# Row maxima of attention scores taken from the transposed scores by 32x32 block transposes

## The chip, the cores and the metric

The kernel runs on one core of a Trainium2 chip. The metric is the device time of one execution in microseconds (us). The core has five engines that work side by side, each through its own queue in order, and that wait for one another through semaphores: TensorE (PE, matmuls into the accumulation memory PSUM), VectorE (DVE), ScalarE (ACT), GpSimd (POOL), and SyncE (SP), which here issues the transfers. PEld is TensorE's load of the stationary operand, which overlaps its matmuls.

## The reference

Two attention layers, one after the other, on 256 positions (16 x 16) of 192 channels. Each layer normalises its input in groups of six channels, computes attention with 12 heads of 16 channels and adds the result to its input. The second layer adds a low-rank term (`A`, `B`) to the weights of q and v. Cut to what matters here:

```python
q, k, v = heads(xn @ W + b)                       # 12 heads, 256 positions, 16 channels
attn = (q * scale) @ k.T                          # 256 x 256 for each head
attn = attn + rel_h[..., :, None] + rel_w[..., None, :]   # from q and the row/column of the key
attn = softmax(attn, axis=-1)
x = x + (attn @ v) @ Wo + bo
```

The softmax subtracts the maximum over the keys from each query's row before the exponential.

## The kernel before

`LAYERS` = 2, `NH` = 12 heads, handled in `PAIRS` = 6 pairs; `NG` = 3 groups of 4 heads for the product with v; `TT` = 2 tiles of 128 positions. PSUM has 8 banks of 512 columns. For every head the operands `qs` and `ks` have 128 rows, which hold q and k in high and low parts and the relative positions, so that one matmul of 128 rows gives the finished scores.

The order of all work is written out by hand: each engine has one list of instructions, and the semaphores are named after what they announce. In the attention part of a layer:

- PE, `scores(l, p)`: scores of pair p with queries as rows (lines 579 on), two heads, two tiles each, into banks 0 and 1 (`S_BANK`). They serve for the maxima alone.
- DVE, `maxima(l, p)`: for each head a reduction of 512 columns to the two tiles' row maxima, negated, into `nm` (line 395).
- POOL, `split_maxima(l, p)`: splits `nm` into a high and a low part in `nmhl` (lines 254 and 256), so that a rounded 32-bit format (fp32r) carries it exactly.
- PE, `turn_max(l, p)`: two matmuls with the identity turn them into rows, in bank 7 (`NM_BANK`, line 605). Bank 7 holds "r" rows of group 2 before (`R_BANK`), so the first waits for the last "r" move.
- ACT, `max_rows(l, p)`: copies these 4 rows into `nmt`.
- PE, `scores_t(l, p)`: the scores again, with keys as rows (line 593), into two pairs of banks in turn (`ST_BANK` = [3, 5]). From the third pair on it waits for the exponentials that empty the banks (`p_sb`).
- PE, `add_max(l, p)`: two matmuls of 512 columns with `ones4` add the negated maxima to the transposed scores (line 615).
- ACT, `probabilities(l, p)`: the exponential of 1024 columns into `pt` (line 316).
- PE, `probs_v(l, g)`: product with v for a group (line 633), then DVE or ACT copies it (`out_columns`, `ot`), `turn_out` turns it back (line 643), and DVE's `normalise` divides by the row sums.

Ahead of this part stand the group norm (DVE's statistics L425, POOL's power L208, DVE's L446 into `xn`), the q, k products (L716), copies into `zq` and `zk` in high parts by ACT and low parts by DVE (L471), the relative positions (L736), and the moves of "k", "q" and "r" rows from PSUM into `ks` and `qs` (ACT's in the order of `ACT_MOVES`, line 268; DVE's, line 380). `keep_busy(n)` issues n small matmuls that have no use but to occupy TensorE. At the start, POOL and DVE fill constants (`ident`, `gavg`, `onehot`, `ones4`, `nmt` and others).

The functions and their callers:

Of the kernel before, what the change touches and what calls it, by code (L numbers as in the profile page):

```python
# [33 lines left out]
def attention_layers(nc, x, w_in0, w_out0, w_in1, w_out1, lora, rel, out):  # L34
# [4 lines left out]
    with ctx:  # L39
# [3 lines left out]
        def sem(name):  # L43
# [17 lines left out]
        ones4_raw = sb("ones4_raw", [P, 2, P])  # L61
        ones4 = sb("ones4", [P, 2, P], F32R)
# [26 lines left out]
        nm = sb("nm", [P, PAIRS, 2, TT])  # L89
        nmhl = sb("nmhl", [P, PAIRS, TT, 2, 2], F32R)  # L90
        nmt = sb("nmt", [P, PAIRS, T], F32R)
# [14 lines left out]
        zeroed, made_ident, made_gavg, made_ones4, made_ones, made_va = (sem(n) for n in (  # L106
            "zeroed", "made_ident", "made_gavg", "made_ones4", "made_ones", "made_va"))
# [4 lines left out]
        (gn_ps, qk_ps, v_ps, rel_ps, k_ps, q_ps, r_ps, s_ps, st_ps, nmt_ps, o_ps, oq_ps, ont_ps,  # L112
         y_ps, lora_ps) = (sem(n) for n in (
            "gn_ps", "qk_ps", "v_ps", "rel_ps", "k_ps", "q_ps", "r_ps", "s_ps", "st_ps", "nmt_ps",
            "o_ps", "oq_ps", "ont_ps", "y_ps", "lora_ps"))

        (warmed, xt_sb, relhi_sb, z_hi, rr_hi_sb, moved_act, nmt_sb, p_sb, ont_sb,
         ot_act, res_act) = (sem(n) for n in (
            "warmed", "xt_sb", "relhi_sb", "z_hi", "rr_hi_sb", "moved_act", "nmt_sb", "p_sb",
# [18 lines left out]
        S_BANK = [0, 1]  # L138
        ST_BANK = [3, 5]
        O_BANK, NM_BANK = [2, 2, 1], 7  # L140
# [10 lines left out]
        BUSY_WITH_MAXIMA = [8, 5]  # L151
# [52 lines left out]
        def _(pool):  # L204
# [25 lines left out]
            for n, steps in enumerate(([-1, 0], [0, -1], [-1, 0], [0, -1])):  # L230
# [5 lines left out]

            pool.memset(va[:, :, :, D:VW], 0.0).then_inc(zeroed, 1)
            pool.memset(ones4_raw[:, :, :], 1.0).then_inc(zeroed, 1)
            pool.wait_ge(zeroed, 11)
            pool.memset(va[:, :, :, D:D + 1], 1.0).then_inc(made_va, 1)  # L240

            pool.affine_select(out=ones4_raw[:, :, :], in_=ones4_raw[:, :, :],
                               compare_op=ALU.is_ge, fill=0.0, base=0, pattern=[[-2, 2], [0, P]],
                               channel_multiplier=1).then_inc(zeroed, 1)
            pool.wait_ge(zeroed, 12)
# [20 lines left out]
        def _(act):  # L266
# [40 lines left out]
            def max_rows(l, p):  # L307

                if l == 0 and p == 0:
                    act.wait_ge(nmt_zero, 1)  # L310
# [521 lines left out]
```

## Time and profile before

| | |
|---|---|
| median of 3 runs | 81.52 us (81.52 to 81.66) |
| profiled execution | 81.54 us |
| its span | 79.5 us |
| PE busy | 69.9 us (88%) |
| PEld busy | 56.0 us (70%) |
| ACT busy | 51.9 us (65%) |
| DVE busy | 45.7 us (58%) |
| POOL busy | 11.8 us (15%) |
| granted TensorE clock, mean | 0.998 of full speed |

The span runs from the first to the last instruction of the profile; the execution's own time has 2.0 us around it. A group row reads: line, engine, operation, result and operands, shapes, number | busy us, mean ns of one | idle time of that engine just before them and what ended it. Matmuls are pipelined: one lasts longer than the distance to the next.

### The profile page before, as it was taken

The numbers are of one execution on the slowest core, as the hardware profiler recorded it, in microseconds if no ns is written. First come the engines' busy times: TensorE is split into PE (matmuls) and PEld (weight loads), VectorE is DVE, ScalarE is ACT, GpSimd is POOL, SyncE is SP. The second block draws the span as 40 slices with busy tenths as digits, with TensorE's granted clock in tenths as the row PEclk, the third lists the DMA queues.
The fourth block names the chain that finished last, engine by engine and source line by source line (L and its number), as shares of the span: only waits on it lengthen the run. The fifth ranks groups of instructions, "written<-read, shape, count | busy, mean of one in ns | idle before, by whom it ended". The sixth has DMA issues, their size and how long they took to land.

```text
span 79.5 us, 1633 instructions
## 1 busy us (share of the span) xinstructions
PE 69.9 (88%) x632; PEld 56.0 (70%) x632; DVE 45.7 (58%) x107; ACT 51.9 (65%) x98; POOL 11.8 (15%) x46
## 2 busy tenths in 40 slices
PE   4976989999978999979999999999878999988750
PEld 4955869998656975824768889999656994834630
DVE  4863999767846685422254649759576666323210
ACT  5429797999979787561330067799979787581420
POOL 5876400000121111000001100000031122000000
PEclk9999999999999999999999999999999999999999
DMA  0968000000000000000000000000000000000003
GB/s 13 278 167 264 12 0 8 0 0 0 0 4 0 8 4 0 0 0 0 0 8 0 0 0 0 0 0 0 8 0 0 0 0 0 0 8 0 0 0 99
DMA packets 1543, 1.75 MB, mean 22 GB/s; under 512 B 312, under 2 KB 1146, under 8 KB 1536
## 3 DMA queue, kind: packets, MB, share of 16 engines
q1 hardware_dynamic: 1536, 1.66, 7.2%
q8 instruction: 5, 0.08, 0.4%
q14 instruction: 2, 0.02, 0.1%
HBM read 1.46 MB, written 0.20 MB: 21 GB/s over the span
## 4 chain that ended last, share of the span: by engine, by line
PE 74%; DVE 10%; ACT 6%; issue 5%; POOL 1%; DVEq 0%; ACTq 0%
PE ps L736 10%; PE ps L633 8%; PE ps L579 7%; PE ps L593 7%; PE ps L615 6%; PE ps L716 6%; PE ps L503 5%; PE ps L564 4%; ACT qs L268 3%; PE ps L643 3%; PE ps L605 2%; PE ps L692 2%; PE ps L536 2%; PE ps L671 2%; PE ps L681 2%
## 5 line engine op out<-in xcount | busy, mean ns | idle before, releaser
L395 DVE TENSOR_REDUCE nm<-ps 128x2 f32<-128x512 f32 x24 | 15.5, 686 | 7.3 <-PE ps L579 7.1
L316 ACT ACTIVATE pt<-ps 128x1024 f32<-128x1024 f32 x12 | 12.3, 1024 | 1.4
L268 ACT ACTIVATE qs<-ps 64x512 fp32r<-64x512 f32 x20 | 11.8, 589 | 0.4
L503 PE MATMUL ps<-busy 128*128 128x128 bf16 x112 | 9.4, 243 | 1.5 <-DVE busy L365 1.1
L503 PEld LDWEIGHTS ps<-busy 128*128 128x128 bf16 x112 | 7.9, 112 | 2.5 <-DVE busy L365 1.0
L579 PE MATMUL ps<-ks,qs 128*128 128x256 f32 x48 | 8.9, 300 | 0.7 <-DVE nm L395 0.3
L736 PEld LDWEIGHTS ps<-zq,table 128*64 128x64 f32 x128 | 7.9, 138 | 0.7 <-issue 0.5
L736 PE MATMUL ps<-zq,table 128*64 128x48 f32 x128 | 8.0, 216 | 0.2 <-DVE zq L471 0.2
L254 POOL CAST nmhl<-nm 128x4 fp32r<-128x4 f32 x12 | 2.2, 187 | 40.1 <-DVE nm L395 40.1
L615 PE MATMUL ps<-nmt,ones 128*128 128x512 f32 x24 | 8.1, 418 | 0.1
L593 PE MATMUL ps<-qs,ks 128*128 128x256 f32 x48 | 8.1, 291 | 0.0
L579 PEld LDWEIGHTS ps<-ks,qs 128*128 128x128 f32 x48 | 6.7, 189 | 1.8 <-issue 0.9
L593 PEld LDWEIGHTS ps<-qs,ks 128*128 128x128 f32 x48 | 6.7, 189 | 1.3 <-issue 0.8
L268 ACT ACTIVATE nmt<-ps 4x256 fp32r<-4x256 f32 x12 | 4.4, 370 | 4.1 <-PE ps L605 3.9
L716 PE MATMUL ps<-xn,win 97*128 97x256 f32 (+1 forms) x24 | 5.7, 387 | 0.8 <-DVE xn L446 0.8
L633 PE MATMUL ps<-pt,va 128*32 128x256 f32 x96 | 6.4, 385 | 0.0
L268 ACT ACTIVATE ks<-ps 64x512 fp32r<-64x512 f32 x10 | 5.7, 589 | 0.1
L478 DVE TENSOR_TENSOR rr_lo<-ps,rr_hi 64x384 fp32r<-64x384 f32 x8 | 4.2, 548 | 2.4 <-ACT rr_hi L268 2.4
L268 ACT ACTIVATE zq<-ps 64x256 fp32r<-64x256 f32 x6 | 2.3, 378 | 5.1 <-PE ps L716 5.0
L716 PEld LDWEIGHTS ps<-xn,win 97*128 97x128 f32 (+1 forms) x24 | 4.4, 189 | 1.5 <-DVE xn L446 1.0
L386 DVE RECIPROCAL rinv<-ps 128x8 f32<-128x8 f32 x6 | 1.2, 208 | 6.0 <-PE ps L643 6.0
L268 ACT ACTIVATE rr_hi<-ps 64x384 fp32r<-64x384 f32 x8 | 3.6, 480 | 1.5 <-PE ps L736 1.4
(94 smaller groups left out, 104.5 us busy)
## 6 DMA issues: line engine op xcount, KB each, us to landing
win<-in_w_in_dram SPq DMA_DIRECT2D x4, 216.0 KB
xt<-in_x_dram SPq DMA_DIRECT2D x1, 192.0 KB, 2.7
wout<-in_w_out_dram SPq DMA_DIRECT2D x2, 96.0 KB
out_dram<-res SPq DMA_DIRECT2D x1, 192.0 KB, 2.0
wout<-in_w_out_dram SPq DMA_DIRECT2D x2, 48.0 KB
rel_raw<-in_rel_dram SPq DMA_DIRECT2D x1, 62.0 KB, 2.9
win<-in_w_in_dram SPq DMA_DIRECT2D x2, 2.2 KB
wout<-in_w_out_dram SPq DMA_DIRECT2D x2, 0.8 KB
```

The source lines that it names most:

```text
L268: return act.activation(dst, src, ACT.Copy, scale=scale)
L316: act.activation(pt[:, p, :, :, :].rearrange("p a k t -> p a (k t)"), ps[:, ST_BANK[p % 2]:ST_BANK[p % 2] + 2, :], ACT.Exp, scale=SCALE[l] ...
L395: dve.tensor_reduce(nm[:, p, a, :], ps[:, S_BANK[a], :].rearrange("p (t k) -> p t k", k=T), AX.X, ALU.max, negate=True).then_inc(max_sb, 1)
L478: dve.tensor_tensor(rel_dst(rr_lo, which, half), rel_src(which, half), rel_dst(rr_hi, which, half).bitcast(F32), ALU.subtract).then_inc(rr ...
L503: mm(ps[:, bank, 0:P], busy[:, :], busy[:, :], start=True, stop=True)
L564: last = mm(ps[:, R_BANK[g], u * T:(u + 1) * T], pick[:, 2 * u:2 * u + 2, :].rearrange("p j n -> p (j n)"), rr[:, g, :], start=(part == 0 ...
L579: last = mm(ps[:, S_BANK[a], t * T:(t + 1) * T], qs[:, 2 * p + a, t * P:(t + 1) * P], ks[:, 2 * p + a, :], start=True, stop=True)
L593: mm(ps[:, ST_BANK[p % 2] + a, t * T:(t + 1) * T], ks[:, 2 * p + a, t * P:(t + 1) * P], qs[:, 2 * p + a, :], start=(t == 0), stop=False, s ...
L615: last = mm(ps[:, ST_BANK[p % 2] + a, :].rearrange("k (t q) -> k t q", q=T), ones4[:, a, :], nmt[:, p, :].unsqueeze(1).to_broadcast([P, TT ...
L633: last = mm(ps[32 * j:32 * j + 32, O_BANK[g], 0:T], va[:, t, G4 * g + j, :], pt[:, 2 * g + j // 2, j % 2, t, :], start=(t == 0), stop=(t = ...
L716: last = mm(ps[:, m, 0:T], win[l][0:rows, ic, m * P:(m + 1) * P], xn[0:rows, ic, :], start=(ic == 0), stop=(ic == 1))
L736: last = mm(ps[0:64, b, c:c + NG * HW], table[l][:, part, which, HW - 1 - i:2 * HW - 1 - i, :].rearrange("p r j -> p (r j)"), moving, star ...
```

## The change

The maxima are taken from the transposed scores. The scores with queries as rows (`scores` before), their banks, and `nmt` with its ACT copies are gone. The new `scores(l, p)` computes what `scores_t` did, into three pairs of banks in turn. `block_tops(l, p, a)` lets VectorE transpose each 32x32 block of one head's scores and reduce it, so that `top` holds for every query the maximum over 32 keys. `turn_tops` turns 16 columns of `top` on PE into bank 7; `maxima` takes the maximum over the 8 blocks of keys, negated, into `nm` (16 rows: head and block of 32 queries; 32 columns). POOL splits `nm` into `nm_hl`, and a new third POOL operation multiplies it with the 0/1 table `place` into `shift`, 256 columns, with every value in its query's column and zeros elsewhere. `subtract_max` adds it to the scores with `ones_rows`. `O_BANK` becomes [2, 0, 1], and the product of group 1 no longer waits for `on` of group 0. `BUSY_WITH_MAXIMA` goes from [8, 5] to 8. At the start DVE computes `place` and `head_rows` and does not clear `nmt`; POOL waits for the normalised input of layer 0 before it clears `va`, `nm_hl` and `shift`, and copies `ones_rows`; the selects of `ones4` go.

```diff
-        S_BANK = [0, 1]
-        ST_BANK = [3, 5]
-        O_BANK, NM_BANK = [2, 2, 1], 7
+        ST_BANK = [0, 3, 5]
+        O_BANK, NM_BANK = [2, 0, 1], 7
-        BUSY_WITH_MAXIMA = [8, 5]
+        BUSY_WITH_MAXIMA = 8
 # POOL
+            pool.wait_ge(xn_sb, NC)
             pool.memset(va[:, :, :, D:VW], 0.0).then_inc(zeroed, 1)
+            pool.memset(nm_hl[:, :, :].bitcast(F32), 0.0).then_inc(shift_zero, 1)
+            pool.memset(shift[:, :, :, :].bitcast(F32), 0.0).then_inc(shift_zero, 1)
+            pool.wait_ge(made_place, 2)
+            pool.tensor_copy(ones_rows[:, :, :], head_rows[:, :].unsqueeze(2).to_broadcast([P, 2, P])
+                             ).then_inc(ones_sb, 1)
             def split_maxima(l, p):
+                n = PAIRS * l + p + 1
+                pool.wait_ge(nm_sb, n)
+                pool.tensor_copy(nm_hl[0:16, p, :], nm[:, p, :]).then_inc(nm_hi, 1)
+                pool.wait_ge(nm_hi, n)
+                pool.tensor_tensor(nm_hl[32:48, p, :], nm[:, p, :], nm_hl[0:16, p, :].bitcast(F32),
                                    ALU.subtract).then_inc(nm_lo, 1)
+                pool.wait_ge(nm_lo, n)
+                if l == 1:
+                    pool.wait_ge(st_ps, p + 1)
+                pool.tensor_tensor(shift[0:48, p, :, :],
+                                   nm_hl[:, p, :].bitcast(F32).unsqueeze(1).to_broadcast([48, 8, 32]),
+                                   place[0:48, :].unsqueeze(2).to_broadcast([48, 8, 32]),
+                                   ALU.mult).then_inc(shift_sb, 1)
 # ACT
-                for n in range(3, 13):
-                    move(l, n)
-                max_rows(l, 0)
-                for n in range(13, 15):
+                for n in range(3, 15):
                     move(l, n)
                 for p in range(PAIRS):
                     probabilities(l, p)
-                    if p == 0:
-                        max_rows(l, 1)
-                    if p + 2 < PAIRS:
-                        max_rows(l, p + 2)
 # DVE
-            dve.memset(nmt[:, :, :].bitcast(F32), 0.0).then_inc(nmt_zero, 1)
+            dve.tensor_reduce(place[:, :], ident[:, :].rearrange("p (x b) -> p b x", b=8),
+                              AX.X, ALU.add).then_inc(made_place, 1)
+            dve.tensor_reduce(head_rows[:, :],
+                              ident[:, 0:64].rearrange("p (s x) -> p s x", s=2)[:, :, 0:16].rearrange(
+                                  "p s (a b) -> p a s b", a=2), AX.XY, ALU.add).then_inc(made_place, 1)
+            def block_tops(l, p, a):
+                dve.wait_ge(s_ps, NH * l + 2 * p + a + 1)
+                if l == 1:
+                    dve.wait_ge(top_ps, p + 1)
+                dve.tensor_reduce(top[:, p, :, a, :],
+                                  ps[:, ST_BANK[p % 3] + a, :].rearrange("p (t b q) -> p t b q", t=TT, q=32),
+                                  AX.X, ALU.max, apply_transpose=True).then_inc(top_sb, 1)
             def maxima(l, p):
+                dve.wait_ge(top_ps, PAIRS * l + p + 1)
+                if l == 1:
+                    dve.wait_ge(nm_lo, p + 1)
+                dve.tensor_reduce(nm[:, p, :],
+                                  ps[0:16, NM_BANK, 0:T].rearrange("p (t b q) -> p q t b", t=TT, q=32),
+                                  AX.XY, ALU.max, negate=True).then_inc(nm_sb, 1)
-                for p in range(PAIRS):
-                    maxima(l, p)
+                block_tops(l, 0, 0)
+                block_tops(l, 0, 1)
+                for p in range(1, PAIRS):
+                    block_tops(l, p, 0)
+                    if p != 3:
+                        maxima(l, p - 1)
+                    block_tops(l, p, 1)
+                    if p == 2:
+                        maxima(l, 2)
                 out_columns(l, 0)
+                maxima(l, 5)
                 normalise(l, 0)
 # PE
+            def scores(l, p):
+                if p == 0:
                     pe.wait_ge(made_keys, 4)
                     moved(l, *(m for g in range(NG) for m in both("k", g)))
                     pe.wait_ge(v_sb, TT * l + 2)
+                elif p >= 3:
+                    pe.wait_ge(p_sb, PAIRS * l + p - 2)
                 moved(l, *both("q", p // 2), *both("r", p // 2))
                 for a in range(2):
                     for t in range(TT):
+                        last = mm(ps[:, ST_BANK[p % 3] + a, t * T:(t + 1) * T],
+                                  ks[:, 2 * p + a, t * P:(t + 1) * P], qs[:, 2 * p + a, :],
+                                  start=(t == 0), stop=(t == 1), skip_group_check=True)
+                    last.then_inc(s_ps, 1)
+            def turn_tops(l, p):
                 if p == 0:
                     moved(l, *both("r", 2))
                 else:
+                    pe.wait_ge(nm_sb, PAIRS * l + p)
+                pe.wait_ge(top_sb, NH * l + 2 * p + 2)
                 for t in range(TT):
+                    last = pe.transpose(ps[0:16, NM_BANK, t * P:(t + 1) * P],
+                                        top[:, p, t, :, :].rearrange("p a b -> p (a b)"), ident[:, :])
+                last.then_inc(top_ps, 1)
+            def subtract_max(l, p):
+                pe.wait_ge(ones_sb, 1)
+                pe.wait_ge(shift_sb, PAIRS * l + p + 1)
                 for a in range(2):
+                    last = mm(ps[:, ST_BANK[p % 3] + a, :].rearrange("k (t q) -> k t q", q=T), ones_rows[:, a, :],
+                              shift[:, p, :, :].rearrange("p b q -> p (b q)").unsqueeze(1).to_broadcast([P, TT, T]),
                               start=False, stop=True, skip_group_check=True)
                 last.then_inc(st_ps, 1)
 # PE, order of a layer's attention part
+                for p in range(3):
+                    scores(l, p)
+                turn_tops(l, 0)
+                turn_tops(l, 1)
+                subtract_max(l, 0)
+                turn_tops(l, 2)
                 moved(l, *both("q", 2))
+                keep_busy(BUSY_WITH_MAXIMA, bank=O_BANK[0])
+                subtract_max(l, 1)
+                scores(l, 3)
+                subtract_max(l, 2)
+                scores(l, 4)
+                turn_tops(l, 3)
+                scores(l, 5)
+                turn_tops(l, 4)
+                subtract_max(l, 3)
+                probs_v(l, 0)
+                turn_tops(l, 5)
+                subtract_max(l, 4)
+                turn_out(l, 0)
+                probs_v(l, 1)
+                subtract_max(l, 5)
+                turn_out(l, 1)
                 probs_v(l, 2)
```

## Rows read from the trace of the kernel before

**Rows 1.** The page: busy time by engine, TensorE's granted clock in 40 slices.

```profile
PE 69.9 (88%) x632; PEld 56.0 (70%) x632; DVE 45.7 (58%) x107; ACT 51.9 (65%) x98; POOL 11.8 (15%) x46
...
PEclk9999999999999999999999999999999999999999
```

**Rows 2.** Timeline, layer 0, attention: start us, us, engine, line, operation.

```profile
18.77 4.28 ACT L268 ACTIVATE qs<-ps 64x512 fp32r<-64x512 f32 x7
...
23.16 0.28 PE L605 MATMUL ps<-ident_r,nmhl 128*4 128x128 f32 x2 [0.54 <-issue]
...
25.03 1.02 ACT L316 ACTIVATE pt<-ps 128x1024 f32<-128x1024 f32 x1
...
33.02 2.18 ACT L316 ACTIVATE pt<-ps 128x1024 f32<-128x1024 f32 x2
...
36.06 1.07 PE L633 MATMUL ps<-pt,va 128*32 128x256 f32 x16
```

**Rows 3.** The chain that ended last, layer 1: start us, us, what.

```profile
72.28 1.04 PE ps L633 x16
```

**Rows 4.** Groups by line with shapes apart.

```profile
L395 DVE TENSOR_REDUCE nm<-ps 128x2 f32<-128x512 f32 x24 | 15.5, 686 | 7.3 <-PE ps L579 7.1
...
L579 PE MATMUL ps<-ks,qs 128*128 128x256 f32 x48 | 8.9, 300 | 0.7 <-DVE nm L395 0.3 <-issue 0.2
...
L615 PE MATMUL ps<-nmt,ones 128*128 128x512 f32 x24 | 8.1, 418 | 0.1
...
L268 ACT ACTIVATE nmt<-ps 4x256 fp32r<-4x256 f32 x12 | 4.4, 370 | 4.1 <-PE ps L605 3.9
...
L605 PE MATMUL ps<-ident_r,nmhl 128*4 128x128 f32 x24 | 3.4, 222 | 1.3 <-issue 1.1
...
L400 DVE COPY ot<-ps 128x256 f32<-128x256 f32 x4 | 1.7, 425 | 4.7 <-PE ps L633 4.7
...
L256 POOL TENSOR_TENSOR nmhl<-nm,nmhl 128x4 fp32r<-128x4 f32 x12 | 2.4, 200 | 1.0
...
L254 POOL CAST nmhl<-nm 128x4 fp32r<-128x4 f32 x12 | 2.2, 187 | 40.1 <-DVE nm L395 40.1
...
L232 POOL TENSOR_SCALAR_AFFINE_SELECT onehot<-onehot 128x256 f32<-128x256 f32 x4 | 2.1, 534 | 0.6
...
L650 PE MATMUL ps<-ident,on 128*64 128x128 f32 x4 | 0.8, 285 | 0.2 <-DVE on L388 0.2
...
L214 POOL TENSOR_SCALAR_AFFINE_SELECT ident<-ident 128x128 f32<-128x128 f32 x1 | 0.3, 289 | 0.2 <-POOL ident L212 0.2
```

**Rows 5.** The chain that ended last: behind a reduction (L395); one pair's scores.

```profile
20.83 0.14 issue
...
27.63 0.48 PE ps L579 x4
```

**Rows 6.** Timeline, start of layer 0.

```profile
0.80 0.38 SPq L162 DMA_DIRECT2D xt<-in_x_dram  x1
...
2.42 1.34 DVE L370 MEMSET nmt<- 128x1536 f32 x1 [0.27 <-issue]
...
3.98 0.74 DVE L425 BATCH_NORM_STATS2 stats<-xt 96x6 f32<-96x256 f32 x2
...
6.99 2.30 ACT L268 ACTIVATE ks<-onehot 64x768 fp32r<-64x768 f32 x3
...
7.43 1.19 DVE L446 TENSOR_SCALAR xn<-xt,gmean,rstd 96x256 f32<-96x256 f32 x2 [0.89 <-POOL rstd L208]
...
10.43 1.32 DVE L471 TENSOR_TENSOR zq<-ps,zq 64x256 fp32r<-64x256 f32 x3
...
11.90 2.02 PE L736 MATMUL ps<-zq,table 128*64 128x48 f32 x32 [0.25 <-DVE zq L471]
```

**Rows 7.** Timeline, start of layer 1, the same L446.

```profile
44.25 0.73 DVE L446 TENSOR_SCALAR xn<-xt,gmean,rstd 96x256 f32<-96x256 f32 x2 [0.37 <-POOL rstd L208]
```

**Rows 8.** DMA issues: KB each, median us from issue to landing.

```profile
xt<-in_x_dram SPq DMA_DIRECT2D x1, 192.0 KB, 2.7
```

More of the change, by code:

```diff
@@ L60, in attention_layers @@
         pick_rl = sb("pick_rl", [P, G4, 64], F32R)
-        ones4_raw = sb("ones4_raw", [P, 2, P])
-        ones4 = sb("ones4", [P, 2, P], F32R)
+        place = sb("place", [P, 8])
+        head_rows = sb("head_rows", [P, 2])
+        ones_rows = sb("ones_rows", [P, 2, P], F32R)
         win = [sb(f"win{l}", [CH + 1, NC, 3 * C]) for l in range(LAYERS)]
@@ L88, in attention_layers @@
         ks = sb("ks", [P, NH, T], F32R)
-        nm = sb("nm", [P, PAIRS, 2, TT])
-        nmhl = sb("nmhl", [P, PAIRS, TT, 2, 2], F32R)
-        nmt = sb("nmt", [P, PAIRS, T], F32R)
+        top = sb("top", [P, PAIRS, TT, 2, 8])
+        nm = sb("nm", [16, PAIRS, 32])
+        nm_hl = sb("nm_hl", [48, PAIRS, 32], F32R)
+        shift = sb("shift", [P, PAIRS, 8, 32], F32R)
         pt = sb("pt", [P, PAIRS, 2, TT, T])
@@ L235, in _ @@
             inverse_deviation(0)
+            pool.wait_ge(xn_sb, NC)
             pool.memset(va[:, :, :, D:VW], 0.0).then_inc(zeroed, 1)
[L238 to L239 removed]
+            pool.wait_ge(zeroed, 10)
             pool.memset(va[:, :, :, D:D + 1], 1.0).then_inc(made_va, 1)
[L242 to L244 removed]
@@ L305, in move @@
                 copy(dst, src).then_inc(moved_act, 1)
-            def max_rows(l, p):
-                if l == 0 and p == 0:
-                    act.wait_ge(nmt_zero, 1)
-                act.wait_ge(nmt_ps, PAIRS * l + p + 1)
-                copy(nmt[0:4, p, :], ps[0:4, NM_BANK, 0:T]).then_inc(nmt_sb, 1)
             def probabilities(l, p):
@@ L316, in probabilities @@
                 act.activation(pt[:, p, :, :, :].rearrange("p a k t -> p a (k t)"),
-                               ps[:, ST_BANK[p % 2]:ST_BANK[p % 2] + 2, :], ACT.Exp,
+                               ps[:, ST_BANK[p % 3]:ST_BANK[p % 3] + 2, :], ACT.Exp,
                                scale=SCALE[l]).then_inc(p_sb, 1)
@@ L567, in relative_rows @@
                 last.then_inc(r_ps, 1)
-            def scores(l, p, heads=(0, 1)):
-                if p == 0 and 0 in heads:
+            def scores(l, p):
+                if p == 0:
                     pe.wait_ge(made_keys, 4)
@@ L573, in scores @@
                     pe.wait_ge(v_sb, TT * l + 2)
+                elif p >= 3:
+                    pe.wait_ge(p_sb, PAIRS * l + p - 2)
                 moved(l, *both("q", p // 2), *both("r", p // 2))
-                for a in heads:
-                    if p >= 1:
-                        pe.wait_ge(max_sb, NH * l + 2 * p + a - 1)
-                    for t in range(TT):
-                        last = mm(ps[:, S_BANK[a], t * T:(t + 1) * T],
-                                  qs[:, 2 * p + a, t * P:(t + 1) * P], ks[:, 2 * p + a, :],
-                                  start=True, stop=True)
-                    last.then_inc(s_ps, 1)
@@ L604, in turn_max @@
                 for t in range(TT):
-                    last = mm(ps[0:4, NM_BANK, t * P:(t + 1) * P],
-                              nmhl[:, p, t, :, :].rearrange("p a s -> p (a s)"), ident_r[:, :],
-                              start=True, stop=True)
-                last.then_inc(nmt_ps, 1)
-            def add_max(l, p):
-                if l == 0 and p == 0:
-                    pe.wait_ge(made_ones4, 1)
-                pe.wait_ge(nmt_sb, PAIRS * l + p + 1)
+                    last = pe.transpose(ps[0:16, NM_BANK, t * P:(t + 1) * P],
+                                        top[:, p, t, :, :].rearrange("p a b -> p (a b)"), ident[:, :])
```

76 lines of the change are left out of this document (10 added, 66 removed).

## The prediction

> **What bounds the kernel now.** I read the page first: TensorE (PE) is busy 88% of the span, VectorE (DVE) 58%, ScalarE (ACT) 65%, GpSimd (POOL) 15%, and the granted clock of TensorE is at full speed, its level of 2.4 GHz, in every slice [rows 1]. That suggests that PE work taken away is time won. The timeline of the attention loop is the test of it. In layer 0 the loop begins with the scores at about 19.6 us. The first turned maxima (L605) come only at 23.16, right after ACT's seventh copy of the stretch that began at 18.77 has ended at 23.05: bank 7, which they write, holds the last "r" rows until then. The first exponentials start at 25.03, the last two end at 35.20 (33.02 + 2.18), and the last `probs_v` starts at 36.06 [rows 2]. In layer 1 the same `probs_v` starts at 72.28 [rows 3], 36.2 us later. So the loop is 16.5 us long per layer, and I judge the change by one mark: when the last `probs_v` starts. What comes after it (copy, turns, projection) is not changed.
>
> **What is removed.** Per pair of heads, PE loses the four matmuls of `scores` (L579; 0.48 us per pair in the chain, 0.12 each, 2.9 us per layer [rows 5]), VectorE loses two reductions to 2 columns of 0.69 us each, ACT loses one 0.37 us copy of `nmt` (2.2 us per layer), and the filler loses 5 of 13 small matmuls (0.3 us) [rows 4]. ACT's copies of the last two "q" rows no longer stand behind the first `nmt` copy.
>
> **What is added, per pair.** (1) Two reductions with 32x32 transposes, 128x512 in each. The reduction of the same input takes 0.69 us [rows 4]; no row shows a transposing one. It reads the same 512 columns, so it cannot be cheaper than 0.69 unless columns stop counting; if a block has to fill before it drains and nothing overlaps, it is about twice the 0.53 us of streaming, 1.2 us. I take 0.72 (one block of 32 columns extra) because the row is the same operation on the same tile; ends 0.69 and 1.2. (2) Two PE transposes of `top`: the nearest form is the turn of `on` with few output columns (L650, 0.285 us each, a pair 0.41), against 0.28 for today's L605 pair. (3) A reduction of 256 columns on 16 partitions: as the 256-column copy from PSUM, 0.42 us; 0.30 at the least. (4) On POOL a copy and a subtraction of 32 columns where there were 4: 0.19 and 0.20 us today [rows 4], which I take as 0.22 and 0.25. (5) A new POOL multiplication into `shift`, 256 columns from two inputs. Selects of 256 columns take up to 0.53 us and one of 128 takes 0.29, which is 1.9 ns a column; 0.20 + 256 x 1.9 ns = 0.69 us. Bounds: 0.41 (a one-input pass of that width, from below) and 1.0 (two such passes). I take 0.69, since the second input has to be read as well. (6) `subtract_max` costs what `add_max` did, 0.68 us for its pair from the first start to the last end.
>
> The Trainium skill's page "GPSIMD Engine Reference", section 3.1, speaks against putting this step on GpSimd: it counts about 2.6 cycles per element for a two-input elementwise operation and 4,497 ns for 2,048 columns, about twice VectorE. [...] No row of this case shows the operation.
>
> **The new chain.** In place of maxima, split (0.47 us on POOL), turn, ACT copy, there is now: block maxima of two heads (1.4 us), +0.11, turn 0.41, maxima 0.42, POOL 0.22 + 0.08 + 0.25 + 0.08 + 0.69 = 1.32, +0.11, subtract 0.68, exponentials 1.02 [rows 4]. For the steps to PE I add 0.11 us, a little under the 0.14 us between the end of a reduction and the next matmul [rows 5], and 0.03 to the others. With the scores (0.5) a pair of banks is held for 6.1 us, and there are three pairs of banks, so a pair of heads comes every 2.0 us at best, as today (the six end 10.2 us after the first starts, so a step is 1.8). The change widens the ring from two to three pairs of banks, and the turn of one grows from 3.6 (two steps of 1.8) to 6.1 us.
>
> Walking layer 0 on the clock of the trace before (order of each engine as in the diff):
> - Scores 0 and 1 at 19.6 and 20.1, block maxima from 20.1. VectorE's queue then holds `maxima(0)`, and `turn_tops(0)` still waits for bank 7 until 23.05, so it starts at 23.16 as L605 does now. VectorE stands still from 22.1 to 23.6 with the rest of pairs 1 and 2 behind it.
> - `maxima(0)` ends at 24.05, POOL at 25.4, subtract 25.5 to 26.2, exponentials 0 from 26.2 to 27.3: 1.2 us later than now.
> - On PE `scores(3)` stands behind `subtract_max(1)`, which gets its shift at 27.2; scores 3 at 27.8, their block maxima end at 29.6, but `maxima(3)` stands behind the first block maxima of pair 4 (29.9 to 30.6). It ends at 31.0, POOL at 32.3, exponentials 3 run from 33.1.
> - Block maxima of pair 5 end at 33.4; `turn_tops(5)` stands behind `probs_v(0)` (32.9 to 33.9). `maxima(5)` ends at 34.85, POOL at 36.2, subtract at 37.0, exponentials 5 at 38.05, `probs_v(2)` starts at 38.2.
>
> So the mark moves from 36.06 to 38.2: 2.1 us per layer, 4.2 us for two. The PE work that went lay beside these waits and buys nothing; ACT's 2.2 us per layer as well.
>
> **The start of layer 0.** VectorE no longer clears `nmt` (1.34 us at 2.42), and does two reductions of about 0.15 instead. It would be ready for the statistics at about 3.1; their input was issued at 0.80 and landed 2.7 later, at 3.5 [rows 8], so they start at 3.57, not 3.98: 0.41 earlier. POOL now clears its tiles only after the normalised input is done. In layer 0, with POOL's memsets beside them, the two L446 take 1.19 us, in layer 1, with POOL still, 0.73 [rows 7]: the first is 0.25 shorter. ACT's first `zq` copy then comes at once after its one-hot copies end at 9.29 (6.99 + 2.30); three of them, 0.4 each, end at 10.5, and the third `zq` subtraction, which today ends at 11.75 (10.43 + 1.32) because VectorE came late to the row, ends at 10.95. PE's L736 starts at 11.1 in place of 11.90: 0.8 us gained [rows 6]. POOL's own new work there (a 1536-column clear, a copy) ends by 11 and nothing waits for it before 20.
>
> **Sum.** The profiled execution: 81.54 us, of which 79.5 are the span. 81.54 + 4.2 - 0.8 = 84.9. The median of the runs is 81.52, the same within 0.02.
>
> **Rivals.**
> - *PE bounds the loop, so its removed work counts* (faster). For: 88% busy, as the page has it. Per layer 2.9 + 0.3 of matmuls go and 6 x 0.13 of longer turns come: 2.4 us, twice, and 0.8: 75.9 at best, and anything up to 81.3 if part of it shows. It decides if the three links maxima, POOL and subtract together are some 0.8 us a pair shorter than the 2.4 above, so that the last exponentials end before 36.3. Against: even with POOL's multiplication at 0.20, as its 4-column row, my walk gives 82.7. Chance 0.09.
> - *The transposing reduction is about half speed* (1.0 to 1.2 us). VectorE then bounds: twelve of them a layer add 0.3 to 0.5 each, and the walk gives 88.4 at 1.0 and 92.0 at 1.2. Nothing in the rows speaks for or against it. Chance 0.12. The Trainium skill's "Vector Engine (DVE) Microarchitecture Reference", section 3.8, has the transposing front end sustain one element per cycle and lane; by that the reduction stays at 0.69 and the sum is 84.7. No row here shows it.
> - *POOL's links are cheap* (multiplication 0.41 to 0.45, maxima 0.30): 82.0 to 83.2, still slower. Chance 0.16.
> - *TensorE's clock falls to 1.2 GHz in the loop*: with fewer matmuls and fewer fillers PE stands idle up to 1.2 us at a time (23.6 to 24.9), and in the profile before the clock never left 2.4 GHz [rows 1], so no row prices it. With matmuls 0.12 us apart becoming 0.24 and all of PE's links doubling, the walk gives 94; a part of it 87 to 90. Chance 0.05. The Trainium skill's "TensorE: Matmul & The Clock Gate" (HAM oscillation) has long idle gaps lower the clock; the trace of before agrees only in that busy stretches keep it.
> - The forecast: chance 0.54, own range 83.2 to 86.6 (multiplication up to 0.9, reduction up to 0.85). No measurable change, within 0.2% (about what a measurement of this kernel can tell from nothing): 0.04, where several links are short at once.
>
> Faster 0.10 (the first rival and a little of the cheap links), same 0.04, slower 0.86. The range for 8 in 10 runs from 81.9 to 88.4: below it lies the first rival, above it the half-speed reduction.
>
> **What would show it.** The transposing reduction at 0.69 to 0.76; POOL's multiplication at 0.6 to 0.8 and POOL as a link of the chain that ended last; VectorE waiting for the first `turn_tops` from about 21.3 to 22.8 (0.8 earlier than on this clock); first exponentials at about 25.4 and last `probs_v` of layer 0 at 37.4; L736 first at 11.1; clock at full. I am wrong if the exponentials keep a step under 1.8 us, or if a step of POOL or of VectorE's new forms lies outside its bounds.

## The result and the profile after

The changed kernel takes 86.55 us (median of 4 runs, 86.27 to 89.18) against 81.52 before: 1.060 times as long, with a 95% interval of 1.056 to 1.064. The profiled execution took 86.37 us, 84.6 of them the span. Executions of one kernel do not all keep TensorE's clock here. So below I read stage lengths from profiled executions and name the granted clock beside the times.

The page after: span, busy time by engine, granted clock in 40 slices.

```profile
span 84.6 us, 1557 instructions
...
PE 68.7 (81%) x574; PEld 51.6 (61%) x574; DVE 48.6 (57%) x120; ACT 47.8 (57%) x86; POOL 20.3 (24%) x58
...
PEclk9999999999975999999999999999955579999999
```

[Rows 1] had 69.9 us of PE. 58 fewer matmuls on TensorE have made it busy for only 1.2 us less, because part of them ran at half speed: the digits of the clock fall to 5 twice, once in each layer's attention loop; before they were 9 throughout. In the chain that ended last (by engine, share of the span) TensorE has 44% where it had 74% before, and ScalarE 29% where it had 6%:

```profile
PE 44%; ACT 29%; DVE 8%; issue 5%; POOL 4%; DMA 4%; SPq 2%; POOLq 1%; DVEq 0%
```

Groups with shapes apart, the counterparts of [rows 4]:

```profile
L392 DVE TRANSPOSE_TENSOR_REDUCE top<-ps 128x16 f32<-128x512 f32 x24 | 15.8, 689 | 4.8 <-PE ps L593 4.6
L315 ACT ACTIVATE pt<-ps 128x1024 f32<-128x1024 f32 x12 | 12.3, 1024 | 16.5 <-PE ps L613 16.3
...
L613 PE MATMUL ps<-shift,ones_rows 128*128 128x512 f32 x24 | 10.3, 518 | 1.3 <-POOL shift L260 1.1
...
L593 PE MATMUL ps<-qs,ks 128*128 128x256 f32 x48 | 8.4, 306 | 3.0 <-ACT qs L274 2.1 <-ACT pt L315 0.6 <-issue 0.2
...
L260 POOL TENSOR_TENSOR shift<-nm_hl,place 48x256 fp32r<-48x256 f32 x12 | 7.3, 608 | 1.0 <-POOL nm_hl L255 0.2
...
L605 PE MATMUL ps<-ident,top 128*16 128x128 f32 x24 | 5.4, 313 | 4.0 <-DVE top L392 3.1 <-ACT qs L274 1.0
L400 DVE TENSOR_REDUCE nm<-ps 16x32 f32<-16x256 f32 x12 | 4.8, 404 | 4.8 <-PE ps L605 4.8
...
L255 POOL TENSOR_TENSOR nm_hl<-nm,nm_hl 16x32 fp32r<-16x32 f32 x12 | 2.9, 243 | 1.0
...
L253 POOL CAST nm_hl<-nm 16x32 fp32r<-16x32 f32 x12 | 2.4, 199 | 40.2 <-DVE nm L400 40.2
```

The transposing reduction takes 0.689 us, as the plain one did (0.686). POOL's multiplication takes 0.608, the maxima 0.404, the widened copy and subtraction 0.199 and 0.243. The means of L613 (0.518) and L605 (0.313) hide two speeds: a part of them ran at the low clock.

The timeline of layer 0's loop (start us, us, engine, line, operation), the counterpart of [rows 2]:

```profile
22.84 0.39 PE L605 MATMUL ps<-ident,top 128*16 128x128 f32 x2 [0.49 <-ACT qs L274]
...
25.17 1.19 PE L613 MATMUL ps<-shift,ones_rows 128*128 128x512 f32 x2
...
26.40 1.02 ACT L315 ACTIVATE pt<-ps 128x1024 f32<-128x1024 f32 x1 [2.38 <-PE ps L613]
...
27.45 0.81 PE L613 MATMUL ps<-shift,ones_rows 128*128 128x512 f32 x2
28.10 0.63 PE L593 MATMUL ps<-qs,ks 128*128 128x256 f32 x4
...
32.98 1.07 PE L627 MATMUL ps<-pt,va 128*32 128x256 f32 x16
33.09 1.02 ACT L315 ACTIVATE pt<-ps 128x1024 f32<-128x1024 f32 x1 [2.61 <-PE ps L613]
...
33.98 0.39 PE L605 MATMUL ps<-ident,top 128*16 128x128 f32 x2
...
35.53 0.61 POOL L260 TENSOR_TENSOR shift<-nm_hl,place 48x256 fp32r<-48x256 f32 x1
...
36.28 0.70 PE L613 MATMUL ps<-shift,ones_rows 128*128 128x512 f32 x2 [0.23 <-POOL shift L260]
...
37.02 1.02 ACT L315 ACTIVATE pt<-ps 128x1024 f32<-128x1024 f32 x1 [1.12 <-PE ps L613]
...
38.10 1.07 PE L627 MATMUL ps<-pt,va 128*32 128x256 f32 x16 [0.90 <-ACT pt L315]
```

The first turn is at 22.84, the first exponentials at 26.40, the last `probs_v` at 38.10, where before they stood at 23.16, 25.03 and 36.06.

Busy time by stretch. A row gives the stretch and its length, then the busy time of PE, PEld, DVE, ACT and POOL, each with its number of instructions, then the granted clock (1.00 is full speed), the DMA share and GB/s. First after, then before for the stretch that leads up to the first exponentials:

```profile
20.60:22.80 2.20, 0.77 (x5) 0.53 (x4) 1.27 (x3) 2.12 (x4) 0.00 (x0) 1.00 0.01 4
22.80:28.00 5.20, 3.80 (x18) 2.31 (x19) 3.08 (x6) 2.21 (x3) 2.59 (x9) 0.67 0.00 0
28.00:38.00 10.00, 8.12 (x64) 4.42 (x62) 6.71 (x15) 5.08 (x5) 3.71 (x10) 1.00 0.01 2
...
61.40:69.00 7.60, 6.31 (x27) 4.42 (x28) 4.39 (x8) 3.32 (x5) 3.15 (x9) 0.55 0.01 2
```

```profile
20.80:25.00 4.20, 3.27 (x18) 2.25 (x18) 3.10 (x6) 3.62 (x7) 0.77 (x4) 1.00 0.01 2
```

Between 20.60 and 22.80 TensorE is busy for 0.77 of 2.20 us, where the kernel before had 3.27 of 4.20. After that the clock falls to its lower level, 1.2 GHz: the mean is 0.67 over 5.2 us in layer 0 and 0.55 over 7.6 us in layer 1. With 0.5 as the lower level these means give an estimate of 3.4 and 6.8 us spent there.

The start of layer 0, the counterpart of [rows 6]:

```profile
3.84 0.75 DVE L431 BATCH_NORM_STATS2 stats<-xt 96x6 f32<-96x256 f32 x2 [0.94 <-DMA xt<-in_x_dram]
...
5.96 0.40 ACT L274 ACTIVATE rel_hi<-rel_raw 128x62 fp32r<-128x62 f32 x2 [3.07 <-DMA rel_raw<-in_rel_dram]
...
7.30 0.73 DVE L452 TENSOR_SCALAR xn<-xt,gmean,rstd 96x256 f32<-96x256 f32 x2 [0.89 <-POOL rstd L209]
7.42 2.30 ACT L274 ACTIVATE ks<-onehot 64x768 fp32r<-64x768 f32 x3
7.77 2.86 PE L710 MATMUL ps<-xn,win 97*128 97x256 f32 x12 [0.58 <-DVE xn L452]
...
9.75 1.19 ACT L274 ACTIVATE zq<-ps 64x256 fp32r<-64x256 f32 x3
10.16 1.32 DVE L477 TENSOR_TENSOR zq<-ps,zq 64x256 fp32r<-64x256 f32 x3 [0.49 <-ACT zq L274]
...
11.63 0.56 PE L730 MATMUL ps<-zq,table 128*64 128x48 f32 x7 [0.35 <-DVE zq L477]
```

The input landed 3.0 us after its issue in this execution instead of 2.7, and the statistics start at 3.84. The two L452 take 0.73, as worked out. ScalarE's first `zq` copy is at 9.75: its row of nine operations begins when the relative positions' input has landed, at 5.96 (5.52 in the profile before). L730 starts at 11.63, 0.27 earlier than before, where 0.8 was forecast. In the profile before, the same copy waited for TensorE's products instead:

```profile
9.73 1.18 ACT L268 ACTIVATE zq<-ps 64x256 fp32r<-64x256 f32 x3 [0.44 <-PE ps L716]
```

To place the 5.1 us between the spans, I use four marks per layer from the timelines. "Loop" is from the first scores to the last `probs_v`.

| | before | after |
|---|---|---|
| first scores, layer 0 | 19.61 | 19.44 |
| loop, layer 0 | 16.45 | 18.66 |
| between the loops | 19.94 | 19.79 |
| loop, layer 1 | 16.21 | 19.47 |
| from the last `probs_v` to the end of the span | 7.29 | 7.24 |

The loops account for 2.21 + 3.26 us; the rest gives 0.4 back.

### The profile page after: what moved, and what is told of

The parts are those of the page before. It is cut to its first block, busy times and chain, and to the rows that moved or that the text cites. A ratio compares the mean times of both kernels' runs of the same rounds, so it can differ in the third digit from the quotient of the medians.

```text
span 84.6 us, 1557 instructions
## 1 busy us (share of the span) xinstructions
PE 68.7 (81%) x574; PEld 51.6 (61%) x574; DVE 48.6 (57%) x120; ACT 47.8 (57%) x86; POOL 20.3 (24%) x58
## 4 chain that ended last, share of the span: by engine, by line
PE 44%; ACT 29%; DVE 8%; issue 5%; POOL 4%; DMA 4%; SPq 2%; POOLq 1%; DVEq 0%
ACT qs L274 11%; PE ps L613 10%; ACT ks L274 9%; PE ps L627 5%; PE ps L730 5%; PE ps L517 4%; DMA rel_raw<-in_rel_dram 4%; PE ps L605 4%; PE ps L710 3%; ACT rr_hi L274 3%; PE ps L593 3%; ACT pt L315 2%; DVE top L392 2%; DVE nm L400 2%; POOL shift L260 2%
## 5 line engine op out<-in xcount | busy, mean ns | idle before, releaser
L315 ACT ACTIVATE pt<-ps 128x1024 f32<-128x1024 f32 x12 | 12.3, 1024 | 16.5 <-PE ps L613 16.3
L392 DVE TRANSPOSE_TENSOR_REDUCE top<-ps 128x16 f32<-128x512 f32 x24 | 15.8, 689 | 4.8 <-PE ps L593 4.6
L253 POOL CAST nm_hl<-nm 16x32 fp32r<-16x32 f32 x12 | 2.4, 199 | 40.2 <-DVE nm L400 40.2
L613 PE MATMUL ps<-shift,ones_rows 128*128 128x512 f32 x24 | 10.3, 518 | 1.3 <-POOL shift L260 1.1
L605 PE MATMUL ps<-ident,top 128*16 128x128 f32 x24 | 5.4, 313 | 4.0 <-DVE top L392 3.1
L730 PEld LDWEIGHTS ps<-zq,table 128*64 128x64 f32 x128 | 7.9, 138 | 0.8 <-issue 0.6
L730 PE MATMUL ps<-zq,table 128*64 128x48 f32 x128 | 8.0, 216 | 0.3 <-DVE zq L477 0.3
L400 DVE TENSOR_REDUCE nm<-ps 16x32 f32<-16x256 f32 x12 | 4.8, 404 | 4.8 <-PE ps L605 4.8
L260 POOL TENSOR_TENSOR shift<-nm_hl,place 48x256 fp32r<-48x256 f32 x12 | 7.3, 608 | 1.0 <-POOL nm_hl L255 0.2
L613 PEld LDWEIGHTS ps<-shift,ones_rows 128*128 128x128 f32 x24 | 4.6, 241 | 3.8 <-issue 3.8
L605 PEld LDWEIGHTS ps<-ident,top 128*16 128x16 f32 x24 | 1.4, 88 | 7.4 <-issue 3.0
L627 PEld LDWEIGHTS ps<-pt,va 128*32 128x32 f32 x96 | 2.5, 109 | 4.4 <-ACT pt L315 2.3
```

The lines of the kernel that those rows point to most:

```text
L260: pool.tensor_tensor(shift[0:48, p, :, :], nm_hl[:, p, :].bitcast(F32).unsqueeze(1).to_broadcast([48, 8, 32]), place[0:48, :].unsqueeze(2) ...
L315: act.activation(pt[:, p, :, :, :].rearrange("p a k t -> p a (k t)"), ps[:, ST_BANK[p % 3]:ST_BANK[p % 3] + 2, :], ACT.Exp, scale=SCALE[l] ...
L392: dve.tensor_reduce(top[:, p, :, a, :], ps[:, ST_BANK[p % 3] + a, :].rearrange("p (t b q) -> p t b q", t=TT, q=32), AX.X, ALU.max, apply_t ...
L400: dve.tensor_reduce(nm[:, p, :], ps[0:16, NM_BANK, 0:T].rearrange("p (t b q) -> p q t b", t=TT, q=32), AX.XY, ALU.max, negate=True).then_i ...
L605: last = pe.transpose(ps[0:16, NM_BANK, t * P:(t + 1) * P], top[:, p, t, :, :].rearrange("p a b -> p (a b)"), ident[:, :])
L613: last = mm(ps[:, ST_BANK[p % 3] + a, :].rearrange("k (t q) -> k t q", q=T), ones_rows[:, a, :], shift[:, p, :, :].rearrange("p b q -> p ( ...
```

## The experiments

**Fillers in the gaps** (`fill`). Small matmuls in unused columns of bank 7, partitions 64 on.

```diff
                 turn_tops(l, 0)
+                for _ in range(18): mm(ps[64:P, NM_BANK, T:T + P], busy[:, 0:64], busy[:, :], start=True, stop=True)
                 turn_tops(l, 1)
+                for _ in range(8): mm(ps[64:P, NM_BANK, T:T + P], busy[:, 0:64], busy[:, :], start=True, stop=True)
                 subtract_max(l, 0)
```

> The changed kernel with 26 filler matmuls per layer in the two gaps of TensorE behind the first and the second turn of the block maxima (64 columns of weights, 128 columns moved, into an unused part of bank 7). If the fall of TensorE's clock to 1.2 GHz in the loop costs the part that the walk of links does not explain (about 1.6 us), the clock stays at 1.00 and the time is 84.6 to 85.4 us. If the clock is a symptom only and the waits set the pace, 86.3 to 86.6. If TensorE's occupied time bounded the loop, it would be slower than the changed kernel, 87.5 or more.

The four executions: 84.24 and 84.14 at a clock of 1.00, 87.33 and 86.91 at 0.96. The windows of the profiled one (84.24), same stretches as above:

```profile
22.80:28.00 5.20, 4.80 (x48) 3.37 (x46) 3.56 (x7) 2.78 (x4) 3.15 (x9) 1.00 0.01 3
...
61.40:69.00 7.60, 6.49 (x54) 4.48 (x51) 5.96 (x11) 3.36 (x4) 3.90 (x12) 1.00 0.00 0
```

The loops are 18.10 and 18.18 us long. With the clock held, the changed kernel is thus 2.1 us faster in spite of 52 more matmuls, so the clock costs 0.56 + 1.29 us in the loops of the profile after, and TensorE's occupied time is not what bounds them. It is still 1.030 times as long as the kernel before (1.024 to 1.037). The other two executions show that fillers of this number do not hold the clock each time. The forecast of 84.6 to 85.4 was 0.4 too high. The second group of fillers stands in the way of the first `subtract_max`: it starts at 25.09, though its shift is ready at 24.80, so the fillers may cost up to 0.2 us of the loop (an estimate).

**Without the multiplication** (`no_mult`). This kernel leaves the maxima unsubtracted (`shift` stays zero) and takes a hundredth of the exponentials' scale.

```diff
-                pool.wait_ge(nm_lo, n)
-                ...
-                pool.tensor_tensor(shift[0:48, p, :, :], ..., ALU.mult).then_inc(shift_sb, 1)
-                pe.wait_ge(shift_sb, PAIRS * l + p + 1)
+                pe.wait_ge(nm_lo, PAIRS * l + p + 1)
```

> The changed kernel without GpSimd's multiplication into shift: the maxima are not subtracted (shift stays zero) and the exponentials take a hundredth of the scale. The chain of links has three multiplications in a row per layer (pairs 0, 3 and 5), each 0.61 us and 0.07 of handover: 6 x 0.68 = 4.1 us less, 82.4 us, and more if TensorE's gaps become short enough to keep the clock (81). If the loop were bound by TensorE's work or by ScalarE, less than 1.5 us would come back: 85 or more.

85.03 us (84.67 to 85.86), clock 0.93 to 0.96: a miss, against 82.4. The loop of layer 0 took 18.73 us, no less than with the multiplication; that of layer 1 took 18.25, 1.2 less. Windows of its layer 0:

```profile
24.00:26.00 2.00, 1.44 (x4) 0.67 (x4) 1.80 (x4) 0.21 (x1) 0.65 (x3) 0.50 0.00 0
26.00:28.00 2.00, 1.88 (x12) 1.68 (x13) 0.41 (x1) 0.81 (x1) 0.44 (x2) 0.50 0.00 0
28.00:30.00 2.00, 2.00 (x8) 1.70 (x7) 1.02 (x2) 1.02 (x1) 0.00 (x0) 0.50 0.00 0
```

The clock is at its lower level from 24 to 30 us. TensorE is busy there for 1.44, 1.88 and 2.00 of each 2.00 us, so from 26 on its own matmuls at half speed fill the time and shorter links can buy little. Clock and link are mixed in this run, and it does not give the price of the link.

**The kernel before without its fillers** (`before_nofill`).

```diff
-        BUSY_WITH_MAXIMA = [8, 5]
+        BUSY_WITH_MAXIMA = [0, 0]
```

> The kernel before without its 13 filler matmuls per layer in the attention loop. If fillers are what holds the clock there, the granted clock falls to about 0.95 and the time rises by 1 us or more, to 82.5 or above. If the loop's own matmuls suffice, the clock stays at 1.00 and the time is 81.0 to 81.6, as 0.6 us of filler per layer lies partly on the chain.

81.55 us, ratio 0.9995 (0.9957 to 1.0032). The page of this kernel:

```profile
span 79.5 us, 1581 instructions
...
PE 69.2 (87%) x606; PEld 54.9 (69%) x606; DVE 45.7 (57%) x107; ACT 51.9 (65%) x98; POOL 11.8 (15%) x46
...
PEclk9999999999999999999999999999999999999999
```

The clock stays up without the fillers, in all ten executions (0.999 or 1.000); the old loop's own matmuls keep it. The kernel before with its fillers, timed beside it, lost the clock in 4 of 13 executions (85.67 to 85.85 us at 0.95 and 0.96), so these fillers are no guarantee. And 0.7 us of TensorE work gone (69.9 to 69.2) change the span by nothing. In the profile before, the fillers stood on the chain that ended last. Being on that chain did not mean that their removal would shorten it: the next item waits for ScalarE's exponentials or VectorE's maxima instead.

**The last r rows first** (`r2_first`, then with fillers `r2_fill`).

```diff
-                     ("q", 0, 0), ("r", 0, 0), ("q", 1, 0), ("q", 1, 1), ("r", 1, 0), ("r", 1, 1),
-                     ("r", 2, 0), ("r", 2, 1), ("q", 2, 0), ("q", 2, 1)]
+                     ("q", 0, 0), ("r", 0, 0), ("r", 2, 0), ("r", 2, 1),
+                     ("q", 1, 0), ("q", 1, 1), ("r", 1, 0), ("r", 1, 1), ("q", 2, 0), ("q", 2, 1)]
-                for p in range(3):
+                for p in range(2):
                     scores(l, p)
                 turn_tops(l, 0)
+                scores(l, 2)
```

> The changed kernel with ScalarE moving the last r rows (group 2) ahead of the q and r rows of group 1, so that bank 7 is free 2.4 us earlier, and the first turn ahead of the scores of pair 2. If the wait for bank 7 holds the loop's start, the first exponentials come about 1.0 us earlier per layer and the time is 84.0 to 85.0. If the ring of three pairs of banks makes up for it later, the last probs_v moves by less than 0.4 per layer and the time is 85.9 or more.

85.26, 84.94, 83.68 and 88.47 us at clocks of 0.94, 0.95, 0.95 and 0.90: the times scatter too much for a verdict. In the profile the first exponentials stand at 24.04, 2.4 us earlier than in the changed kernel (5.0 us behind the first scores instead of 7.0), and the loops are 18.05 and 17.87 long, 0.6 and 1.6 shorter, at a clock that still falls.

> ScalarE moves the last r rows first and the first turn stands ahead of the scores of pair 2, now with fillers in the gaps (18 and 10 per layer). With the clock at 1.00 the wait for bank 7 should be worth about 1.0 us per layer: 82.3 against 84.2 for the filled kernel. If the ring makes up for it, 83.8 or more.

In `r2_fill` fillers stand behind the first turn (18) and behind the first subtract (10). The loops are 17.13 and 17.28 us, at a clock of 1.00 within them: 0.97 and 0.90 shorter than in `fill`, as forecast. The time of that execution was 85.59 all the same. Its page's clock row:

```profile
PEclk9999999999999999999995558999999999999999
```

The dip has moved to the stretch between the loops (44 to 51 us), which took 22.94 us instead of the 19.80 of `fill`. TensorE had been busy without a break from 36.4 to 44 us ahead of this fall, so it is not gaps just before it that brought it on. Without the 3.14 us the profiled execution would have come to 82.45 (an estimate). The one execution with the clock at 1.00 took 83.61, where 82.3 was expected. It has no profile, and that difference stays open.

**Without the multiplication, with fillers** (`no_mult_fill`): both edits together, maxima unsubtracted again.

> The filled kernel (26 filler matmuls per layer, which held the clock at 1.00 in its profile) without GpSimd's multiplication: the maxima are not subtracted and the exponentials take a hundredth of the scale. With the clock held, the price of this link should show by itself. A multiplication is 0.61 us; the first run without it had the clock at 0.94 and told little. If all of pairs 0, 3 and 5 are on the chain, 6 x 0.68 = 4.1 us less than the filled kernel's 84.2: 80.1. If the last subtract stands behind probs_v(1) anyway, as that run's timeline suggests, and ScalarE's moves hold the first exponentials, only about 0.8 per layer comes back: 82.6.

82.22 us in the execution at a clock of 1.00, the others 84.16 to 84.81 at 0.96 to 0.97. In the profile the loop of layer 0 ran at the full clock and took 17.10 us, 1.0 less than in `fill` (layer 1 lost the clock). The best executions differ by 2.0 us for two layers (84.24 and 82.22). So the second branch holds: in this order the link is worth about 1 us a layer and not 2, since `subtract_max(5)` then stands behind `probs_v(1)` on TensorE (34.66, then 35.66). The first exponentials gain nothing, 6.75 us behind the first scores in both kernels: there the first subtraction waits for `turn_tops(1)` and the eight fillers behind it. The 1 us is thus what the link costs with these fillers in place, and could be more without them.

**The best order found** (`best_order`), on top of `r2_fill`:

```diff
                 turn_tops(l, 3)
+                probs_v(l, 0)
                 scores(l, 5)
                 turn_tops(l, 4)
                 subtract_max(l, 3)
-                probs_v(l, 0)
                 turn_tops(l, 5)
-                subtract_max(l, 4)
                 turn_out(l, 0)
+                subtract_max(l, 4)
                 probs_v(l, 1)
```

> As the one with the last r rows first and fillers, and on TensorE probs_v(0) goes into the gap ahead of scores 5, and the turn of pair 5 ahead of the subtract of pair 4, so that nothing but its own links holds the last exponentials. Working the links through with the measured durations gives another 0.4 per layer: 81.4, the time of the kernel before within 0.5. If the links are bound elsewhere (VectorE's row of block maxima), 82.3 as without it.

81.34 us at a clock of 1.00, 83.00 to 83.05 at 0.98. The loops are 16.79 and 16.83, another 0.34 and 0.45 less than in `r2_fill`, as forecast, at the full clock; the profiled execution (83.00) lost its clock between the loops.

**The relative positions' input issued second**, in three kernels: with the best order (`best_rel`), in the changed kernel (`after_rel`), and in the kernel before with the start of the change (`before_start_rel`). A fourth, `before_start`, has the same start with the input in its old place, behind the first weights.

```diff
             sp.dma_start(xt[0][:, :, :], x.rearrange("(k p) t -> p k t", p=CH)).then_inc(ld_x, 16)
+            sp.dma_start(rel_raw[:, :, :], rel).then_inc(ld_rel, 16)
```

The start of the change in the kernel before. It is not all of it: the selects of `ones4` stay.

```diff
             inverse_deviation(0)
+            pool.wait_ge(xn_sb, NC)
             ...
+            pool.memset(nmt[:, :, :].bitcast(F32), 0.0).then_inc(nmt_zero, 1)
-            dve.memset(nmt[:, :, :].bitcast(F32), 0.0).then_inc(nmt_zero, 1)
```

> The same, with the relative positions' input issued second instead of fifth. The chain of the changed kernel begins with that transfer (landed at 5.94 us) and ScalarE's nine operations behind it, up to the first zq copy at 9.75. If ScalarE is what is late there, it starts 0.3 to 0.6 us earlier and the time falls as much, to 81.0. If TensorE's products (from 7.77) hold the zq copies, or the weights now land later, no change or slower.

81.20 us median (80.92 to 83.14, 9 runs), ratio 0.9925 (0.9881 to 0.997): the only version with the new maxima that the runs show ahead of the kernel before, by 0.75%, counted over the six executions that kept the clock. Three of the nine lost it and took 82.92 to 83.14. Its profiled execution, 80.92 us:

```profile
span 79.1 us, 1669 instructions
...
PEclk9999999999999999999999999999999999999999
```

The first scores start at 18.46 instead of 19.02 in `best_order`; the loops (16.81, 16.77) are the same. TensorE's products, which the first `zq` copy follows 1.6 us later in both, begin at 7.26 instead of 7.82. That is the whole 0.56 us, so this pair does not show that the moved transfer gave it.

> The changed kernel with the relative positions' input issued second. If ScalarE's wait for it (until 5.96 us) is what held the start, L730 starts at 10.7 to 10.9 instead of 11.63 and the loop 0.8 us earlier, 85.5 us; the clock falls in the loop as before. If something else held it, 86.4.

ScalarE's row now begins at 3.60, and L730 at 10.98 instead of 11.63 (timeline of this kernel):

```profile
3.60 0.40 ACT L274 ACTIVATE rel_hi<-rel_raw 128x62 fp32r<-128x62 f32 x2 [0.70 <-DMA rel_raw<-in_rel_dram]
...
7.50 2.86 PE L710 MATMUL ps<-xn,win 97*128 97x256 f32 x12 [0.58 <-DVE xn L452]
...
9.10 1.18 ACT L274 ACTIVATE zq<-ps 64x256 fp32r<-64x256 f32 x3 [1.26 <-PE ps L710]
...
10.98 1.20 PE L730 MATMUL ps<-zq,table 128*64 128x48 f32 x18
```

So that input did hold the start of the changed kernel: the first `zq` copy now waits for TensorE's products and no longer for ScalarE's own row. Not all of the 0.65 us is its doing. The products begin 0.27 earlier (7.50 for 7.77), as the other input landed earlier in this execution; 0.38 is left for the moved transfer. The time did not follow, and the forecast of 85.5 missed: 86.24 to 87.57 us at clocks of 0.92 to 0.94, ratio 1.062 (1.051 to 1.073) to the kernel before. The loops are 19.03 and 19.45 long and the stretch between them 21.40, with the clock down in all three.

> The kernel before with the start of the change alone: GpSimd instead of VectorE clears nmt, and waits for the normalised input before it clears anything. The prediction gave this 0.8 us; the changed kernel showed TensorE's L730 only 0.27 us earlier, because ScalarE stood behind the input of the relative positions. If that is the reason, the time falls by 0.2 to 0.5 here too (81.0 to 81.3), and by as much as the landing of that input varies. If the gain is lost again before the loop because ScalarE's moves set the first turn, 81.5.

82.79 to 85.18 us at clocks of 0.95 to 0.98 in all four executions, against a forecast of 81.0 to 81.3, while the loops kept their 16.35 and 16.36. This run is inconclusive on the 0.8 us. In its profile the stretch between the loops takes 22.95 instead of 19.94, with the clock down from 44 to 52 us. The first scores come at 20.45, 0.84 later than in the kernel before: the L718 products take 3.88 us where `before_start_rel` has 2.86, and the 17 fillers ahead of them 1.97 against 1.11. Yet the granted clock in the windows is 1.00 (the row of the fillers in `before_start`, then in `before_start_rel`, then the window of `before_start`):

```profile
6.37 1.97 PE L505 MATMUL ps<-busy 128*128 128x128 bf16 x17
...
5.96 1.11 PE L505 MATMUL ps<-busy 128*128 128x128 bf16 x17
...
6.00:8.00 2.00, 2.00 (x21) 2.00 (x20) 0.57 (x3) 1.98 (x6) 0.70 (x1) 1.00 0.80 257
```

So in the first microseconds TensorE can be slow without the granted clock showing it. `no_mult_fill` has the same slow start (first scores at 20.39). Whether this lies behind the 83.61 of `r2_fill` at a clock of 1.00 is not shown.

> The same with the relative positions' input issued second. With ScalarE early as well, the full 0.8 us and some more should show: 80.2 to 80.7. Beside the version with the new maxima, the best order, fillers and this same start (80.92 to 81.2), it tells what the new maxima are worth at their best: that version's loop is 16.8 us a layer against 16.4, so this one should be 0.6 to 0.9 us faster than it.

80.72 us median (80.54 to 80.86 at a clock of 1.00, one at 82.92 and 0.98), ratio 0.9865 (0.9799 to 0.9931), as forecast at its upper end. The first scores are at 19.21, 0.40 earlier than in the kernel before, the loops 16.42 and 16.37. It is 0.5 us faster than `best_rel` by the medians of all executions and 0.6 by those that kept the clock (80.59 and 81.18), where 0.6 to 0.9 was forecast; the intervals of the two ratios overlap. The loops show it better: 32.79 us for both layers against 33.58, so the old maxima are still 0.8 us ahead of the new ones at their best. The two profiled executions differ by only 0.06 us in all, because the starts are not the same: `best_rel` has its first scores 0.75 earlier.

## Why the prediction was right, and where it was off

The direction and the range held: 86.55 lies in 81.9 to 88.4. The point, 84.9, was 1.65 too low. Against the profiled execution (86.37) it was 1.5 too low, and the marks divide that: the clock in the loops +1.85, the start +0.63, the links -0.58, and the other stretches with the time outside the span about -0.5. That the result lies even in the forecast's own range of 83.2 to 86.6 is in part luck: that range assumed the full clock, and errors of both signs stand in the sum. With the clock held the kernel took 84.2, 0.7 below the point.

- **The loop's links** (forecast +2.1 us a layer). With the clock held they measure +1.65 in layer 0 (18.10 against 16.45) and +1.97 in layer 1 (18.18 against 16.21). The mechanism was right: the turn of the banks by way of VectorE, TensorE, VectorE, POOL and TensorE takes longer than the work it relieves. Of the 1.65 us, 1.0 goes when the multiplication goes (`no_mult_fill`), and 0.97 when bank 7 comes free early and the first turn moves up (`r2_fill`); the two were not taken out together. In the timeline `turn_tops(5)` at 33.98 does stand behind `probs_v(0)`, and scores 3 (28.10) behind `subtract_max(1)` (27.45). The terms were a little too large: the multiplication 0.608 for 0.69, the maxima 0.404 for 0.42, the copy 0.199 for 0.22, the reduction 0.689 for 0.72. The Trainium skill's "GPSIMD Engine Reference" (section 3.1) has 4,497 ns for 2,048 columns of such an operation, which makes an estimate of 0.56 us for 256 columns with nothing fixed added; the measured 0.608 lies just above it. The Trainium skill's "Vector Engine (DVE) Microarchitecture Reference" (section 3.8) has the transposing front end sustain one element per cycle and lane; the trace agrees, as the reduction takes 0.689 us with the transposes and 0.686 without.
- **The start** (forecast 0.8 us gained). The first scores moved by 0.17. The step that failed is "ACT's first `zq` copy then comes at once after its one-hot copies end at 9.29": it took their end as fixed, and they begin behind a transfer. That transfer was 0.44 later in this profile, and its issue is not moved by the change. `after_rel` shows that this was the cause: with the transfer issued earlier the copy waits for the products instead. By that run about 0.4 us of the start is the transfer's.
- **TensorE's clock** (a rival with 0.05, priced at 94 for the whole loop and 87 to 90 for a part of it). It happened in every execution timed of the changed kernel, clock 0.92 to 0.94, and costs about 2 us. The lower level held for some 3.4 of 18.7 us in layer 0 and 6.8 of 19.5 in layer 1, and the median of 86.55 lies below even the price for a part. The sign that I had in hand was weighed too lightly: my walk had VectorE and TensorE both waiting for bank 7, and four matmuls a pair gone. This is the largest part of the miss.
- **The other rivals.** "PE bounds the loop" is refuted: in `fill`, at the full clock, the loops are 1.65 and 1.97 us longer than before though the 24 matmuls of the old scores are gone from each, and in `before_nofill` less work gave nothing. A half-speed reduction did not occur, and neither did cheap links on POOL (0.608 for a multiplication of 0.41 to 0.45, 0.404 for maxima of 0.30).
- **The signs.** The reduction and the multiplication came out as named. The first exponentials (26.40 for 25.4), the last `probs_v` (38.10 for 37.4), L730 (11.63 for 11.1) and the full clock did not; with the clock held (`fill`) the last `probs_v` is at 37.22.
- ScalarE's 2.2 us of `nmt` copies a layer went and the loop got longer, as forecast: it now idles 16.3 us in front of the exponentials, which wait for L613. No run takes these copies away alone.

What stays open: what decides in which executions, and where, the clock falls. In the loop the gaps matter: without the added fillers all 16 executions of kernels with the new maxima lost the clock, with them 14 of 25, and in the profile of `fill` both loops kept it. But gaps are not all of it. The kernel before lost the clock in 6 of the 33 executions timed beside the experiments, `before_start` in four of four with the same loops, and in `r2_fill` it fell between the loops after 7 us without a gap.

## What to carry to other kernels

Work taken off the busiest engine can buy nothing where that engine stands in a ring of short waits: count the links from the moment a buffer fills until it is free again, divide by the number of buffers, and compare that with the present step. Look for an in-order instruction that must wait early in the loop (here for a bank that ScalarE frees late in its row); moving that copy first, and the first turn ahead of the third scores, was worth 0.9 to 1.0 us a layer at the full clock. Treat gaps on TensorE as a cost of their own: a change that opens them should be timed with the granted clock beside each execution.

## What the runs showed of the hardware

- A reduction of 128x512 fp32 from PSUM with 32x32 transposes takes 689 ns, the plain one 686 ns: the transpose costs nothing that can be told.
- GpSimd's two-input operation on 48x256 fp32 takes 608 ns, on 16x32 243 ns, on 128x4 200 ns: an estimate of 1.6 ns for each further column, from rows with different numbers of partitions.
- VectorE's two L446 take 1.19 us with GpSimd's memsets beside them and, as L452 of the changed kernel, 0.73 us without.
- Two subtract matmuls of 512 columns take 0.70 us from the first start to the last end at the full clock and 1.19 at 1.2 GHz.
- 17 small matmuls near 6 us take 1.97 us in one execution and 1.11 in another, with a granted clock of 1.00 in both (`before_start`, `before_start_rel`).
